# Elementwise work of keys, values, second layernorm and probability lows at fixed steps of VectorE, with GpSimd left to start transfers

## The chip, the core and the metric

The kernel runs on one core of a Trainium2 chip. The metric is the device time of one execution in microseconds (us); several executions are made, and their median is given. The profile names TensorE's matmuls PE and its weight loads PEld, VectorE DVE, ScalarE ACT, GpSimd POOL and SyncE SP.

## The reference

Sixteen sequences of 128 tokens, 1024 wide, pass through one block: cross attention behind a layernorm, then a linear layer with a routed low-rank addition behind a second layernorm.

```python
...
_layernorm(x) = (x - mean(x)) / sqrt(var(x) + 1e-05)
...
q = apply_rope((query @ Wq).reshape(b, t, 32, 128))
k = apply_rope((key @ Wk).reshape(b, t, 8, 128))
v = (value @ Wv).reshape(b, t, 8, 128)
logits = jnp.einsum('btkgd,bTkd->bkgtT', q, k) * ATTN_MULT
logits = MAX_ATTN_VAL * jnp.tanh(logits / MAX_ATTN_VAL)
logits = jnp.where(mask, logits, -1e+30)
attn = jnp.einsum('bkgtT,bTkd->btkgd', softmax(logits), v)
return attn.reshape(b, t, h * d) @ Wo
...
rw, sel = jax.lax.top_k(xf @ W_router.T, 2)
w = jnp.einsum('tk,tke->te', softmax(rw), onehot(sel))
lora = jnp.einsum('ter,te,eor->to', einsum('td,erd->ter', xf, A), w, B) * SCALING
return xf @ W_base.T + b_base + lora
...
x = x + cross_attention(_layernorm(x), ctx_4096, mask)
x = x + ffn(_layernorm(x))
```

## The kernel before, in words

All is float32. A product of two float32 matrices is made as three matmuls on rounded parts: each operand is split into a high part, copied by ScalarE into the type fp32r, and a low part, the float32 value less the high part, a subtraction on VectorE or GpSimd. `three()` (L233) issues high x high (L235), high x low (L236) and low x high (L237). So almost every tile that reaches TensorE costs one copy and one subtraction first, and elementwise work is spread over the three other engines.

The order of every engine is written out by hand. Each phase has a function per engine (`pe_kv`, `act_kv`, `dve_kv`, `pool_kv`, `sp_kv` and so on) that walks over the same job or step numbers; tables say which extra work stands at which number. `tick` counts a named semaphore up when an instruction ends, `wait_ge` makes an engine wait for such a count; every engine executes in order, so all that stands behind a waiting instruction waits too.

The 2048 tokens are four blocks of 512 columns (4 sequences each); `c` is the block.

**Keys and values (0 to some 325 us).** 56 jobs n of 24 matmuls write seven PSUM banks in turn. VectorE follows one or two jobs behind: the rotation of the keys (L386 to L400), the low part of the values (`vst`, L538), and the statistics of the first layernorm of x (`BN_STATS`, L547). `STATS`, `RS_A`, `RS_B`, `DIAG`, `SPREAD` say at which job number n the parts of that layernorm stand. `MASK` is 28: at this job TensorE makes a small product with the mask (L433) that is built into the bound `Bm` on the scores; VectorE has cast the mask before, at n = 26 (`mf`, `mr`, L591 and L593). `SUMS` are four instructions each on VectorE (L617 to L622), which add normalised blocks `Yx` of x in pairs to `T`, for a query product with seven products in place of eight. GpSimd makes the low part of the keys (`kst`) for the first eight pairs (`KPOOL`) and normalises the blocks `Yx` (one addition, L638, one multiplication, L643), and starts their stores to `XcD`. It has no job numbers there: each instruction runs as soon as its waits allow.

**Queries (some 328 us to the first attention steps).** The change leaves these functions as they are.

**Attention (some 960 to 1927 us).** 32 groups gi (four blocks c, eight key heads) of four query heads b. Steps `at` run from -16 to 255; a group takes eight steps. For head b of a group: scores, `tanh` on ScalarE, the minimum with `Bm` on VectorE (L1486), `exp` to `Pf`, copy to the high part `Ph`, low part `Pl` on GpSimd (L1528). At `DEN_AT` TensorE sums the probabilities of the group with a product with ones (L1291, 8 matmuls). The sums go through a transfer to `r`, a reciprocal on VectorE (L1498) one step later, a store to `rD` and a transfer `RB` per head that spreads the reciprocals over the partitions (L1519); all three are started by GpSimd. Five to ten steps behind the sums the products with the values are made, multiplied by `RB` (L1492), and split into `Ah` and `Al` (L1466). The same step of TensorE holds one job of the output product, 128x512, whose result VectorE adds into one of eight blocks of `Y` (L1479), with the job eight steps earlier in the same block. The weights of that product are 128x1024 pieces, split into `Rh` (L1216) and `Rl` (L1221).

In `dve_step` the order within a step is: low part of the queries `ql`, `Al`, addition into `Y`, minimum with `Bm`, product with `RB`, `Rl`, reciprocal.

**Second layernorm.** When a block c is done (every 64 steps), its layernorm is made during the next 64 steps, r = at % 64. `LN_LOAD` (4) to `LN_OUT` (38) are the values of r: sum over the rows (`ln_sum`), mean by a product with ones, subtraction of it (`ln_x`, L1790), squares on ScalarE, their sum (`ln_acc`, L1796), the root, one step of Newton (`ln_r`), multiplication (`ln_u`, L1813), and the split into high and low (`ln_xl`, L1774). GpSimd has 35 of these instructions per block, one `ln_x` per step and one `ln_u` every second step among them. The fourth block has the same steps squeezed into the jobs J of the second matrix product by `ln_last(J)`.

**Second matrix product (from 1928 us).** 40 jobs J of 24 matmuls, each with its router and low-rank parts. `r_lo` copies (L2033) a part of the router's weights that TensorE's first small product (L1885) needs.

```python
SUMS = {25: (0, 0), 26: (0, 1), 33: (0, 2), 35: (0, 3)}
KPOOL = 8
...
for d in (1, 2):
    if at - d in DEN_AT:
        gi = DEN_AT[at - d]
        for b in (2 * d - 2, 2 * d - 1):
            x = 4 * gi + b
```

Of the kernel before, what the change touches and what calls it, by code (L numbers as in the profile page):

```python
# [97 lines left out]
def program(nc, xT, xN, ctxT, gran, mask, bias, cst, dram, out):  # L98
    kD, vD, vE, qD, XcD, QSD, X2D, x1D, rD = dram
    ctx = ExitStack()  # L100
    with ctx:
# [259 lines left out]
        SUMS = {25: (0, 0), 26: (0, 1), 33: (0, 2), 35: (0, 3)}  # L361
# [5 lines left out]

        YLOAD = {2: 0}
# [131 lines left out]
        KPOOL = 8  # L500

        def k_low(t, u):

            for s in range(2):
                t.wait_ge("kv_kh", (u, s))
                t.e.tensor_tensor(kst[s][:, 1, :], kt[2 * (u % 2) + s][:, :], f(kst[s][:, 0, :]), ALU.subtract).then_inc(
                    *(t.tick("kv_kl", (u, s)) if u >= KPOOL else t.tick("kv_kp", (u, s))))

        def dve_kv(t):
# [5 lines left out]
            for n in range(-1, NK + 3):  # L515
# [78 lines left out]
                if n == MASK + 1:  # L594
# [30 lines left out]
        def pool_kv(t):  # L625
            e = t.e
            for u in range(KPOOL):
                k_low(t, u)
            for cp in range(1):
                for k, i in ((0, 0), (1, 0), (0, 1), (1, 1), (2, 0), (2, 1), (3, 0), (3, 1)):  # L630
                    b, s = xl0 if i == 0 else xl1
                    if (k, i) == (2, 0):
                        t.wait_ge("kv_lo", piece_of["W", 15])
                    for kk in (k, k + 4):
                        y = Yx[i][:, kk, :]
                        t.wait_ge(f"d_yx{i}{kk // 2}", cp)
                        t.wait_ge("kv_x", (2 * cp + i, 0))
                        e.tensor_tensor(y, y, b[:, :], ALU.add).then_inc(*t.tick("kv_xa", (cp, k, i, kk // 4)))  # L638
                    for kk in (k, k + 4):
                        y = Yx[i][:, kk, :]  # L640
                        t.wait_ge("kv_x", (2 * cp + i, 1))
                        t.wait_ge("kv_xa", (cp, k, i, kk // 4))
                        m = e.tensor_tensor(y, y, s[:, :], ALU.mult)  # L643
                        m.then_inc(*(t.tick("kv_xm", (cp, k, i)) if kk < 4 else t.tick("kv_xn", (cp, k, i))))
                    t.wait_ge("kv_xn", (cp, k, i))
                    for n, kk in ((0, k), (2, k + 4)) if i == 0 else ((6, k + 4),):
                        if k > 1:
                            t.wait_ge(f"d_xs{k % 2}{n}", (cp, k - 2))
                        e.dma_start(XcD[cp, n, :, k], Yx[i][:, kk, :]).then_inc(*t.tick(f"d_xs{k % 2}{n}", (cp, k), 16))
# [804 lines left out]
        def dve_step(t, at):  # L1454
# [38 lines left out]
            for x in [y for y in SPLIT.get(at, []) if at >= 0]:  # L1493
                w_low(t, x)
            if at - 1 in DEN_AT:
                gi = DEN_AT[at - 1]
                t.wait_ge(f"d_rt{gi % 2}", gi)
                e.reciprocal(r16[gi % 2][:, :], r16[gi % 2][:, :]).then_inc(*t.tick("a_rec", gi))  # L1498
            dve_ln(t, at)

        def pool_step(t, at):
# [19 lines left out]
            for d in (1, 2):  # L1521
                if at - d in DEN_AT:
                    gi = DEN_AT[at - d]
                    for b in (2 * d - 2, 2 * d - 1):
                        x = 4 * gi + b
                        t.wait_ge("a_ph", x)
                        t.wait_ge("a_den", gi)
                        e.tensor_tensor(Pl[x % NP][:, :], Pf[x % NP][:, :], f(Ph[x % NP][:, :]), ALU.subtract).then_inc(*t.tick("a_pl", x))  # L1528
# [6 lines left out]
            if 11 <= at < 19:  # L1535
                n = at - 11
                t.wait_ge("y_add", n + 8)
                t.wait_ge(f"d_y{n // 2}", 0)
                e.tensor_tensor(Y[:, n, :], Y[:, n, :], Y2[:, n, :], ALU.add).then_inc(*t.tick("y_x", n))
            pool_rows(t, at)  # L1540
            pool_ln(t, at)

        def pool_rows(t, at):
# [3 lines left out]
            if at - 2 < 0 or n < 0:  # L1547
                return
            o = at - 2 - n
            if n:  # L1550
                t.wait_ge("y_add", at - 2)
                if n == 1:
                    if c:
                        t.wait_ge("ln_u", (c - 1, 7))
                    else:
                        t.wait_ge("q_xm", (3, 3))
                    e.tensor_tensor(L2[:, :], Y[:, 0, :], Y[:, 1, :], ALU.add).then_inc(*t.tick("ln_sum", (c, 1)))
                else:
# [665 lines left out]
```

## Time and profile before

| | before |
|---|---|
| time, median of 3 runs | 2170.22 us (2169.26 to 2170.89) |
| the profiled execution | 2171.35 us |
| its span in the profile | 2169.6 us |
| granted clock of TensorE, mean | 0.997 |
| PE, PEld busy | 98%, 79% |
| DVE, ACT, POOL busy | 76%, 40%, 36% |
| DMA, mean rate | 234 GB/s |

The busy time is a sum over the whole span; it does not say whether the work was in anyone's way. A wait of an engine is given with the instruction that released it. Matmuls overlap in the timeline: one lasts some 0.4 us from its start to its end while the next starts earlier, so the pace is the distance of the starts. A granted clock of 1.0 is 2.4 GHz.

### The profile page before, as it was taken

The page shows a single profiled execution, that of the slowest core. Times are in us where ns is not written, and L with a number is a line of the kernel's source. Part 1 is how long each engine was busy: PE and PEld are TensorE (multiplying, and loading weights), DVE is VectorE, ACT ScalarE, POOL GpSimd, SP SyncE. Part 2 cuts the span into 40 slices and gives each one's busy share as a digit, 9 for nine tenths or more (in the row PEclk, how much of TensorE's full clock was granted, in tenths as well). Part 3 has the DMA queues.
Part 4 walks back from the last instruction along what each step waited for, and adds up shares of the span by engine and source line. Part 5 has one row for each costly group of instructions (what it writes and reads, how often), then busy time and mean ns, then how long its engine had stood idle before and what let it go on. Part 6 is the DMA issues. An engine that isn't in the chain of part 4 may idle for free.

```text
span 2169.6 us, 26526 instructions
## 1 busy us (share of the span) xinstructions
PE 2132.5 (98%) x9429; PEld 1723.6 (79%) x9429; DVE 1642.6 (76%) x2062; ACT 869.4 (40%) x1351; POOL 772.8 (36%) x761
## 2 busy tenths in 40 slices
PE   9998999999999999998999999999999999999999
PEld 7887887888788888876777777777777777888887
DVE  5957758898987666675777789898999989855533
ACT  3323333222241111146555556665565556423221
POOL 0371016555540000004533455445645554525300
PEclk9999999999999999999999999999999999999999
DMA  8678667777686565677655575578456855586861
GB/s 323 224 247 261 211 228 275 265 277 258 247 317 241 209 214 199 227 265 245 219 197 184 196 281 194 195 253 309 149 192 238 303 191 166 196 347 240 313 224 59
DMA packets 198532, 508.52 MB, mean 234 GB/s; under 512 B 20864, under 2 KB 46080, under 8 KB 196352
## 3 DMA queue, kind: packets, MB, share of 16 engines
q1 hardware_dynamic: 172160, 424.43, 55.3%
q0 software_dynamic: 26240, 82.38, 11.4%
q8 instruction: 76, 1.25, 0.2%
q14 instruction: 56, 0.46, 0.1%
HBM read 357.26 MB, written 149.16 MB: 233 GB/s over the span
## 4 chain that ended last, share of the span: by engine, by line
PE 85%; DVE 7%; issue 4%; DMA 2%; ACT 1%; POOL 1%; SPq 0%; DVEq 0%; ACTq 0%; POOLq 0%
PE pq L235 28%; PE pq L236 27%; PE pq L237 27%; PE pq L1291 1%; DVE ql L1373 1%; DVE Rl L1221 1%; DVE Y L1479 1%; DVE Al L1466 1%; DVE pq L1492 1%; DVE pq L1486 1%; DMA kraw<-ctxT 1%; POOL Pl L1528 0%; PE pq L1885 0%; DMA vD<-vst 0%; PE pq L1886 0%
## 5 line engine op out<-in xcount | busy, mean ns | idle before, releaser
L235 PE MATMUL pq<-Ah,Rh 128*128 128x512 f32 x1024 | 400.8, 391 | 7.4 <-DVE Y L1479 3.9
L237 PE MATMUL pq<-Ah,Rl 128*128 128x512 f32 x1024 | 399.3, 390 | 0.0
L236 PE MATMUL pq<-Al,Rh 128*128 128x512 f32 x1024 | 399.2, 390 | 0.0
L1221 DVE TENSOR_TENSOR Rl<-raw,Rh 128x1024 fp32r<-128x1024 f32 x176 | 274.0, 1558 | 122.3 <-ACT Rh L1216 121.9
L235 PE MATMUL pq<-Xq,qW 128*128 128x512 f32 x896 | 349.9, 391 | 4.9 <-issue 3.8
L236 PE MATMUL pq<-Xq,qW 128*128 128x512 f32 x896 | 349.3, 390 | 0.0
L237 PE MATMUL pq<-Xq,qW 128*128 128x512 f32 x896 | 349.2, 390 | 0.0
L1216 ACT ACTIVATE Rh<-raw 128x1024 fp32r<-128x1024 f32 x176 | 184.6, 1050 | 152.8 <-PE pq L237 119.7
L235 PEld LDWEIGHTS pq<-Ah,Rh 128*128 128x128 f32 x1024 | 192.6, 188 | 53.4 <-DVE Y L1479 5.8
L1534 POOL DMA_DIRECT2D r<-rT x32 | 22.9, 716 | 575.8 <-ACT rT L1402 575.8
L237 PEld LDWEIGHTS pq<-Ah,Rl 128*128 128x128 f32 x1024 | 192.5, 188 | 40.7
L236 PEld LDWEIGHTS pq<-Al,Rh 128*128 128x128 f32 x1024 | 192.7, 188 | 39.9
L235 PEld LDWEIGHTS pq<-Xq,qW 128*128 128x128 f32 x896 | 168.5, 188 | 42.9 <-issue 7.0
L237 PEld LDWEIGHTS pq<-Xq,qW 128*128 128x128 f32 x896 | 168.6, 188 | 35.2
L236 PEld LDWEIGHTS pq<-Xq,qW 128*128 128x128 f32 x896 | 168.6, 188 | 34.7
L1479 DVE TENSOR_TENSOR Y<-pq,Y 128x512 f32<-128x512 f32 x248 | 168.7, 681 | 34.8 <-PE pq L237 34.5
L869 ACT ACTIVATE qW<-qraw 128x512 fp32r<-128x512 f32 x96 | 60.6, 632 | 294.0 <-PE pq L237 267.2
L1373 DVE TENSOR_TENSOR ql<-qf,qh 128x512 fp32r<-128x512 f32 x128 | 174.6, 1365 | 0.0
L1528 POOL TENSOR_TENSOR Pl<-Pf,Ph 128x512 fp32r<-128x512 f32 x128 | 164.1, 1309 | 1.1
L1394 ACT ACTIVATE Ah<-pq 128x512 fp32r<-128x512 f32 x128 | 76.1, 594 | 141.7 <-DVE pq L1492 141.5
L1408 ACT ACTIVATE Pf<-pq 128x512 f32<-128x512 f32 x128 | 76.5, 598 | 117.8 <-DVE pq L1486 117.5
L1388 ACT ACTIVATE pq<-pq 128x512 f32<-128x512 f32 x128 | 74.9, 585 | 111.1 <-PE pq L237 110.7
(244 smaller groups left out, 4188.5 us busy)
## 6 DMA issues: line engine op xcount, KB each, us to landing
raw<-gran SPq DMA_DIRECT2D x177, 512.0 KB, 4.5
QSD<-qW SPq DMA_DIRECT2D x64, 512.0 KB, 3.4
qD<-qt SPq DMA_DIRECT2D x128, 256.0 KB, 5.5
qW<-QSD SPq DMA_DIRECT2D x64, 512.0 KB, 3.5
qf<-qD SPq DMA_DIRECT2D x64, 512.0 KB, 6.3
RB<-rD POOLq DMA_DIRECT2D x128, 256.0 KB, 4.9
qraw<-gran SPq DMA_DIRECT2D x48, 512.0 KB, 5.1
kD<-kst SPq DMA_DIRECT2D x32, 512.0 KB, 5.4
```

The source lines that it names most:

```text
L235: e.matmul(dst, lh, rh, start=first, stop=False, skip_group_check=more)
L236: e.matmul(dst, lh, rl, start=False, stop=False, skip_group_check=more)
L237: return e.matmul(dst, ll, rh, start=False, stop=last, skip_group_check=more)
L869: e.activation(q_place(u)[:, 0, :], q_source(u), ACT.Copy).then_inc(*t.tick("q_hi", u))
L1216: t.e.activation(piece(x)[1], raw[raw_of(x)][:, :], ACT.Copy).then_inc(*t.tick("w_hi", x))
L1221: t.e.tensor_tensor(l, raw[raw_of(x)][:, :], f(h), ALU.subtract).then_inc(*t.tick("w_lo", x))
L1373: t.e.tensor_tensor(v4(ql[x % 2][:, :]), qf[gi % 2][:, :, b * P:b * P + P], f(v4(qh[x % 2][:, :])), ALU.subtract).then_inc(*t.tick("a_ql", x))
L1388: e.activation(s, s, ACT.Tanh, scale=SCALE / CAP).then_inc(*t.tick("a_tanh", x))
L1394: e.activation(Ah[:, 4 * i:4 * i + 4, b * P:b * P + P], v4(ps[obank[x % 2]][:, :]), ACT.Copy).then_inc(*t.tick("a_ah", x))
L1408: e.activation(Pf[x % NP][:, :], s, ACT.Exp, scale=CAP).then_inc(*t.tick("a_exp", x))
L1479: e.tensor_tensor(Y[:, m, :], ps[ring_bank(n)][:, :], Y[:, m, :], ALU.add).then_inc(*t.tick("y_add", n))
L1528: e.tensor_tensor(Pl[x % NP][:, :], Pf[x % NP][:, :], f(Ph[x % NP][:, :]), ALU.subtract).then_inc(*t.tick("a_pl", x))
```

## The change

It moves 324 elementwise instructions of 128x512 from GpSimd to VectorE, each to a fixed step: 128 `Pl`, 16 `kst`, 32 on `Yx`, 8 additions of the residual into `Y` (`y_x`), and 140 of the second layernorm (the fourth block's too). GpSimd keeps the start of every transfer that it had. The first two `SUMS` go from jobs 25 and 26 to 26 and 27 and stand, as before, behind the mask casts in the code of one job number. `LN_OUT` goes from 38 to 39. The four `Pl` of a group stand 1, 2, 4 and 6 steps behind `DEN_AT` (1, 2, 2, 2 in the first three groups), ahead of the reciprocal. `ln_x` stand at r = 9, three at 11, and one each at 12 to 15. The last block's layernorm reaches to J = 22 instead of 17, and its reload starts at J = 24 instead of 22.

```diff
-        SUMS = {25: (0, 0), 26: (0, 1), 33: (0, 2), 35: (0, 3)}
+        SUMS = {26: (0, 0), 27: (0, 1), 33: (0, 2), 35: (0, 3)}
...
+        XBLOCK = {20: (0, 0), 21: (1, 0), 22: (0, 1), 25: (1, 1), 28: (2, 0), 29: (2, 1), 30: (3, 0), 31: (3, 1)}
...
-        KPOOL = 8
...
                     u = pair_of[KJ[n - 2][1:3]]
-                    if u >= KPOOL:
-                        k_low(t, u)
+                    k_low(t, u)
...
+                if n in XBLOCK:
+                    k, i = XBLOCK[n]
+                    m, s = xl0 if i == 0 else xl1
+                    for kk in (k, k + 4):
...
+                        e.tensor_tensor(y, y, m[:, :], ALU.add).then_inc(*t.tick("kv_xa", (0, k, i, kk // 4)))
+                    for kk in (k, k + 4):
...
+                        p = e.tensor_tensor(y, y, s[:, :], ALU.mult)
...
         def pool_kv(t):
             e = t.e
-            for u in range(KPOOL):
-                k_low(t, u)
...
+            for k, i in XBLOCK.values():
+                t.wait_ge("kv_xn", (0, k, i))
...
+                    e.dma_start(XcD[0, n, :, k], Yx[i][:, kk, :]).then_inc(*t.tick(f"d_xs{k % 2}{n}", (0, k), 16))
...
+        PL_AT = {}
+        for at, gi in DEN_AT.items():
+            for b, d in enumerate((1, 2, 2, 2) if gi < 3 else (1, 2, 4, 6)):
+                PL_AT.setdefault(at + d, []).append((gi, b))
...
                 w_low(t, x)
+            for gi, b in PL_AT.get(at, []):
+                x = 4 * gi + b
+                t.wait_ge("a_ph", x)
+                t.wait_ge("a_den", gi)
+                e.tensor_tensor(Pl[x % NP][:, :], Pf[x % NP][:, :], f(Ph[x % NP][:, :]), ALU.subtract).then_inc(*t.tick("a_pl", x))
             if at - 1 in DEN_AT:
...
+            if 11 <= at < 19:
...
+                e.tensor_tensor(Y[:, n, :], Y[:, n, :], Y2[:, n, :], ALU.add).then_inc(*t.tick("y_x", n))
+            if at == NT - 4:
+                r_lo(t, 0)
+            dve_rows(t, at)
             dve_ln(t, at)
...
-        LN_LOAD, LN_MEAN, LN_SQUARE, LN_SPLIT, LN_RSTD, LN_MORE, LN_OUT = 4, 8, 15, 25, 30, 36, 38
+        LN_LOAD, LN_MEAN, LN_SQUARE, LN_SPLIT, LN_RSTD, LN_MORE, LN_OUT = 4, 8, 15, 25, 30, 36, 39
+
+        LN_X = {9: (0,), 11: (1, 2, 3), 12: (4,), 13: (5,), 14: (6,), 15: (7,)}
...
-            if LN_MEAN + 1 <= r < LN_MEAN + 9:
-                k = r - LN_MEAN - 1
+            for k in LN_X.get(r, ()):
...
         def dve_ffn(t):
             e = t.e
-            r_lo(t, 0)
+            for at in (NT + 1, NT + 2):
+                dve_rows(t, at)
...
-                if J == 22:
+                if J == 24:
                     f_load(t, C - 1)
```

The order of the instructions on VectorE around the mask casts, before (`T` are the sums of `SUMS`, `vst` is the low part of a value job, `mf` and `mr` the casts of the mask):

```order
L549 BN_AGGR mv<-bnst 128x2
L617 TENSOR_TENSOR T_71<-Yx_68,Yx_67 128x512
L618 TENSOR_TENSOR T_73<-Yx_68 128x512
L620 TENSOR_TENSOR T_72<-Yx_68,T_71 128x512
L622 TENSOR_TENSOR T_74<-Yx_67,T_72 128x512
L538 TENSOR_TENSOR vst_106<-pq,vst_106 128x512
L547 BN_STATS bnst<-xn_70 128x6 x2
L549 BN_AGGR mv<-bnst 128x2
L591 CAST mf<-mu_107 128x128
L593 CAST mr<-mf 128x128
```

and with the change:

```order
L547 BN_AGGR mv<-bnst 128x2
L612 TENSOR_TENSOR Yx_68<-Yx_68,D_59 128x512 x2
L617 TENSOR_TENSOR Yx_68<-Yx_68,D_60 128x512 x2
L536 TENSOR_TENSOR vst_106<-pq,vst_106 128x512
L545 BN_STATS bnst<-xn_70 128x6 x2
L547 BN_AGGR mv<-bnst 128x2
L589 CAST mf<-mu_107 128x128
L591 CAST mr<-mf 128x128
L629 TENSOR_TENSOR T_71<-Yx_68,Yx_67 128x512
L630 TENSOR_TENSOR T_73<-Yx_68 128x512
L632 TENSOR_TENSOR T_72<-Yx_68,T_71 128x512
L634 TENSOR_TENSOR T_74<-Yx_67,T_72 128x512
```

The first `SUMS` are behind the casts now, and four instructions on `Yx`, which GpSimd had, are ahead of them.

VectorE in attention, around the reciprocal of a group, at r = 11 of a layernorm (`Y_158` is the block of `ln_x`, `r_56` the reciprocal), before:

```order
L1373 TENSOR_TENSOR ql_150<-qf_160,qh_148 128x512
L1479 TENSOR_TENSOR Y<-pq,Y 128x512
L1492 TENSOR_TENSOR pq<-pq,RB 128x512
L1221 TENSOR_TENSOR Rl_167<-raw_172,Rh_163 128x1024
L1498 RECIPROCAL r_56<-r_56 128x16
L1466 TENSOR_TENSOR Al<-pq,Ah 128x4x128
L1479 TENSOR_TENSOR Y<-pq,Y 128x512
L1486 TENSOR_TENSOR pq<-pq,Bm 128x512
```

and with the change:

```order
L1772 TENSOR_TENSOR Y_158<-Y_158,L_57 128x512 x3
L1372 TENSOR_TENSOR ql_150<-qf_160,qh_148 128x512
L1478 TENSOR_TENSOR Y<-pq,Y 128x512
L1491 TENSOR_TENSOR pq<-pq,RB 128x512
L1220 TENSOR_TENSOR Rl_167<-raw_172,Rh_163 128x1024
L1498 TENSOR_TENSOR Pl_185<-Pf_192,Ph_178 128x512
L1502 RECIPROCAL r_56<-r_56 128x16
L1772 TENSOR_TENSOR Y_158<-Y_158,L_57 128x512
L1465 TENSOR_TENSOR Al<-pq,Ah 128x4x128
L1478 TENSOR_TENSOR Y<-pq,Y 128x512
L1485 TENSOR_TENSOR pq<-pq,Bm 128x512
```

Between `Bm` and the reciprocal stand three `ln_x` and one `Pl` more, and a `Pl` or an `ln_x` stands in each step.

GpSimd over the same steps, before; of these rows those with DMA are left with the change:

```order
L1534 DMA r_56<-rT_153 128x1x16
L1790 TENSOR_TENSOR Y_158<-Y_158,L_57 128x512
L1528 TENSOR_TENSOR Pl_185<-Pf_192,Ph_178 128x512
L1528 TENSOR_TENSOR Pl_186<-Pf_193,Ph_179 128x512
L1790 TENSOR_TENSOR Y_158<-Y_158,L_57 128x512
L1509 DMA rD<-r_56 128x16
L1528 TENSOR_TENSOR Pl_187<-Pf_194,Ph_180 128x512
L1528 TENSOR_TENSOR Pl_188<-Pf_195,Ph_181 128x512
L1790 TENSOR_TENSOR Y_158<-Y_158,L_57 128x512
L1519 DMA RB<-rD 128x512 x4
L1790 TENSOR_TENSOR Y_158<-Y_158,L_57 128x512 x3
```

The chain from `r` over `rD` to `RB` has no arithmetic of GpSimd between its starts any more.

## Rows read from the trace of the kernel before

**Rows 1.** Page, part 1: busy us, share of span, instructions of each engine.
```profile
PE 2132.5 (98%) x9429; PEld 1723.6 (79%) x9429; DVE 1642.6 (76%) x2062; ACT 869.4 (40%) x1351; POOL 772.8 (36%) x761
```

**Rows 2.** Waits of TensorE: us in total, times, longest.
```profile
PE pq L433 <- DVE mr L593: 7.8, 1, 7.8
PE pq L235 <- DVE Y L1479: 3.9, 4, 1.2
...
PE pq L1885 <- DVE Rh L2033: 1.1, 1, 1.1
```

**Rows 3.** Timeline of VectorE, 156 to 172 us: start, us, engine, line, operation, names, shapes.
```profile
156.89 5.99 DVE L618 TENSOR_TENSOR T<-Yx 128x512 f32<-128x512 f32 x1
...
169.13 0.68 DVE L538 TENSOR_TENSOR vst<-pq,vst 128x512 fp32r<-128x512 f32 x1
...
171.36 0.23 DVE L593 CAST mr<-mf 128x128 fp32r<-128x128 f32 x1
171.51 0.68 DVE L617 TENSOR_TENSOR T<-Yx,Yx 128x512 f32<-128x512 f32 x1
172.11 0.69 DVE L618 TENSOR_TENSOR T<-Yx 128x512 f32<-128x512 f32 x1
```

**Rows 4.** Timeline of GpSimd, 156 to 163 us; x2: two in a row.
```profile
157.29 2.55 POOL L638 TENSOR_TENSOR Yx<-Yx,L 128x512 f32<-128x512 f32 x2
```

**Rows 5.** Groups of VectorE, shapes apart: busy us, mean ns, idle us before.
```profile
L1221 DVE TENSOR_TENSOR Rl<-raw,Rh 128x1024 fp32r<-128x1024 f32 x176 | 274.0, 1558 | 122.3 <-ACT Rh L1216 121.9
L1373 DVE TENSOR_TENSOR ql<-qf,qh 128x512 fp32r<-128x512 f32 x128 | 174.6, 1365 | 0.0
...
L1498 DVE RECIPROCAL r<-r 128x16 f32<-128x16 f32 x32 | 7.7, 242 | 13.0 <-DMA r<-rT 13.0
...
L1221 DVE TENSOR_TENSOR Vl<-raw,Vh 128x1024 fp32r<-128x1024 f32 x4 | 4.9, 1217 | 0.0
```

**Rows 6.** Timeline of TensorE, 171 to 172 us; in brackets the idle time before.
```profile
171.65 0.47 PE L433 MATMUL pq<-mr,ones 128*128 128x128 f32 x1 [7.79 <-DVE mr L593]
```

**Rows 7.** Two windows: us, busy (x) of PE, PEld, DVE, ACT, POOL, granted clock, DMA share.
```profile
160.00:180.00 20.00, 12.21 (x47) 9.66 (x46) 18.83 (x20) 5.15 (x8) 8.90 (x9) 0.83 0.54 183
180.00:200.00 20.00, 20.00 (x90) 16.57 (x89) 11.70 (x26) 6.19 (x8) 0.00 (x0) 1.00 0.86 261
```

**Rows 8.** Timeline of ScalarE, 156 to 158 us.
```profile
157.36 0.60 ACT L495 ACTIVATE vst<-pq 128x512 fp32r<-128x512 f32 x1 [4.90 <-DMA vD<-vst]
```

**Rows 9.** Chain that ended last: start, us, instructions; the ones products.
```profile
1057.03 1.00 PE pq L1291 x8
...
1114.40 1.00 PE pq L1291 x8
1142.83 1.00 PE pq L1291 x8
...
1864.33 1.00 PE pq L1291 x8
```

**Rows 10.** Timeline of TensorE, 1043 to 1053 us.
```profile
1043.43 0.47 PE L235 MATMUL pq<-Ah,Rh 128*128 128x512 f32 x1 [0.73 <-DVE Al L1466]
...
1052.41 0.50 PE L235 MATMUL pq<-Ah,Rh 128*128 128x512 f32 x1 [1.93 <-ACT Y L1415]
```

**Rows 11.** Timeline of all engines, 1332 to 1334 us.
```profile
1332.36 2.14 POOL L1519 DMA_DIRECT2D RB<-rD  x4 [0.73 <-DMA rD<-r]
...
1333.30 1.21 DVE L1221 TENSOR_TENSOR Rl<-raw,Rh 128x1024 fp32r<-128x1024 f32 x1
```

**Rows 12.** Timeline of VectorE, 1926 to 1928 us.
```profile
1926.79 0.69 DVE L1479 TENSOR_TENSOR Y<-pq,Y 128x512 f32<-128x512 f32 x1 [1.69 <-PE pq L237]
1927.40 0.18 DVE L2033 CAST Rh<-Rl 128x64 fp32r<-128x64 f32 x1
```

**Rows 13.** Timeline of VectorE, 1507 to 1508 us.
```profile
1507.60 0.70 DVE L1492 TENSOR_TENSOR pq<-pq,RB 128x512 f32<-128x512 f32 x1 [2.54 <-DMA RB<-rD]
```

More of the change, by code:

```diff
@@ L626, in pool_kv @@
             e = t.e
-            for u in range(KPOOL):
-                k_low(t, u)
[L629 to L649, printed above, removed]
+            for k, i in XBLOCK.values():
+                t.wait_ge("kv_xn", (0, k, i))
+                for n, kk in ((0, k), (2, k + 4)) if i == 0 else ((6, k + 4),):
+                    if k > 1:
+                        t.wait_ge(f"d_xs{k % 2}{n}", (0, k - 2))
+                    e.dma_start(XcD[0, n, :, k], Yx[i][:, kk, :]).then_inc(*t.tick(f"d_xs{k % 2}{n}", (0, k), 16))
             for c, half, b4 in v_jobs:
@@ L1520, in pool_step @@
             v_store(t, at)
[L1521 to L1528, printed above, removed]
             if at in DEN_AT:
@@ L1534, in pool_step, with dve_rows @@
                 e.dma_start(r16[gi % 2][:, :], rT[gi % 2][0:P:32, :]).then_inc(*t.tick(f"d_rt{gi % 2}", gi, 16))
[L1535 to L1539, printed above, removed]
             pool_rows(t, at)
             pool_ln(t, at)
+        def dve_rows(t, at):
+            e = t.e
+            c, n = (at - 2) // 64, (at - 2) % 64 - 56
+            if at - 2 < 0 or n < 1:
+                return
+            t.wait_ge("y_add", at - 2)
+            if n == 1:
+                if c:
+                    t.wait_ge("ln_u", (c - 1, 7))
+                else:
+                    t.wait_ge("q_xm", (3, 3))
+                e.tensor_tensor(L2[:, :], Y[:, 0, :], Y[:, 1, :], ALU.add).then_inc(*t.tick("ln_sum", (c, 1)))
+            else:
+                t.wait_ge("ln_sum", (c, n - 1))
+                e.tensor_tensor(L2[:, :], L2[:, :], Y[:, n, :], ALU.add).then_inc(*t.tick("ln_sum", (c, n)))
         def pool_rows(t, at):
@@ L1546, in pool_rows @@
             c, n = (at - 2) // 64, (at - 2) % 64 - 56
[L1547 to L1550, printed above, removed]
+            if at - 2 > 0 and n > 0 and n % 2:
                 t.wait_ge("y_add", at - 2)
[L1552 to L1558, printed above, removed]
-                    t.wait_ge("ln_sum", (c, n - 1))
-                    e.tensor_tensor(L2[:, :], L2[:, :], Y[:, n, :], ALU.add).then_inc(*t.tick("ln_sum", (c, n)))
-            if n % 2:
                 j = n // 2
@@ L1807, in pool_ln_step @@
                 e.tensor_tensor(L2[:, :], Dt[0][:, :], Dt[1][:, :], ALU.mult).then_inc(*t.tick("ln_r", (c, 2)))
+            if LN_OUT + 2 <= r < LN_OUT + 18 and (r - LN_OUT) % 2 == 0:
+                k = (r - LN_OUT) // 2 - 1
+                t.wait_ge("ln_xh", (c, k))
+                e.tensor_tensor(stg[k % 2][:, 1, :], Dt[k % 2][:, :], f(stg[k % 2][:, 0, :]), ALU.subtract).then_inc(*t.tick("ln_xl", (c, k)))
             if LN_OUT <= r < LN_OUT + 16 and (r - LN_OUT) % 2 == 0:
```

66 lines of the change are left out of this document (37 added, 29 removed).

## The prediction

> **What bounds the kernel now.** I read the page first: TensorE is busy 98% of the span [rows 1]. Shortening another engine's work therefore gains nothing by itself; only a stop of TensorE, or a stretch at its lower clock, can be won back. So the second view is TensorE's list of waits. Three entries bear on the change [rows 2]: 7.8 us once on VectorE's mask cast `mr`, 3.9 us in four waits on the accumulation `Y`, 1.1 us on the copy `Rh` at the start of the second matrix product. The rest stands in places that the change leaves alone.
>
> The third view says why VectorE was late. At the mask wait one subtraction of 128x512 whose operands both lie in SBUF took 5.99 us, while the same instruction 15 us later took 0.69, starting 0.60 after its neighbour [rows 3]. In those 5.99 us GpSimd ran one elementwise instruction of 1.3 us behind the other on the same kind of data [rows 4]. The same shows in the means: `Rl` takes 1558 ns where the like `Vl`, made while GpSimd rests, takes 1217, and `ql` takes 1365 [rows 5].
>
> **Part 1, keys, values and the mask.** TensorE would begin the mask product at 163.86 (171.65 less 7.79) [rows 6]. The wait costs more than its length: in the window that holds it 47 matmuls stand against 90 in the next and the granted clock is 0.83 [rows 7], so for some matmuls behind the stop TensorE ran at 1.2 instead of 2.4 GHz. 43 missing matmuls by 20/90 us are 9.6 us. The change takes all elementwise work off GpSimd there, and puts the first `SUMS` behind the mask casts in VectorE's order. What VectorE must then do between ScalarE's copy of value job 25, which ends at 157.96 [rows 8], and the end of `mr` is what it did from 169.13 to 171.59 [rows 3], 2.46 us. That gives 160.4, which is 3.4 us before TensorE comes. The four `Yx` instructions now ahead of it at step 25 (4 x 0.60 = 2.4 us) end before that copy does. If they and a late transfer met, up to 3.4 us would still be hidden. Term: **-9.6 us**, between -9.6 and about -4 (the casts late by 5 us more). The 16 `kst` instructions add 16 x 0.60 = 9.6 us to VectorE over the first 110 us; TensorE writes seven banks in turn there and VectorE follows one or two jobs behind, so I cost them at nothing. If that cover went, 9.6 us is the most. The transfers begun by GpSimd there keep their order and only come free of the arithmetic.
>
> **Part 2, attention.** The sum of ones products marks a period of the steady part: 28.43 us undisturbed (1114.40 to 1142.83). From the first shown, 1057.03, to the last, 1864.33, there are 28 periods, 796.0 us at that pace, and the three layernorm passes add 12 matmuls of 20/90 us, 2.7 us [rows 7]; 807.3 passed [rows 9]. So 8.6 us are lost there, more than the 3.9 us that the waits on `Y` say, because each stop also has a slow restart. What VectorE must do in a period, undisturbed, is four `Rl` of 1.22, 24 instructions of 0.60 (four each of `Bm`, `RB`, `Al` and `ql`, eight `Y`) and a reciprocal of 0.24, 19.5 us [rows 3, 5]. The change adds four `Pl`: 21.9. In the fullest periods of layernorm, 8 more instructions (`ln_u`, `ln_xl`, or `ln_x`, whose spread is the same) make 26.7 of 28.43 us, 94%. Over the kernel 324 instructions move, 324 x 0.60 = 194 us; what VectorE gets back is (1.558 - 1.217) x 176 + (1.365 - 0.69) x 128 = 146 us, and the smaller groups [rows 3, 5]. On average it is about as busy as now, but no single instruction lasts 5 us. TensorE needs an addition into `Y` only two steps (7.1 us) after VectorE may begin it, and the worst single step of the new order holds 4.5 us against 28.43 / 8 = 3.55, with lighter ones around it. So stops of this kind should end; I leave 1.6 us for new small ones. Term: **-7 us**, bounds -8.6 and 0.
>
> The start of attention does not gain. There VectorE waits for the broadcast `RB`, and TensorE stands 1.93 us at 1052.41 for what follows on it [rows 10]; this chain of transfers is started at the same events as before. Three `Pl` now lie ahead of `Al`, for which TensorE waited 0.73 us at 1043.43; they make that wait 1.8 us longer, and the 1.93 us behind it shorter by as much. Term 0, bounds -2 and +2. Beginning transfers costs GpSimd what it did, 2.14 / 4 = 0.53 us for each of four `RB` even beside a `Rl` of VectorE [rows 11].
>
> Here the Trainium skill speaks against the change: by "SBUF — State Buffer", section "SBUF: two separate sides", a VectorE instruction in a 2-port mode locks GpSimd out of writing descriptors, so that a start of some 620 ns takes 3100. It would hold for copies and casts; the same page, "Who interferes with whom", says that `tensor_tensor` stalled no transfer, and by that rule the trace agrees with its 0.53 us. By the first rule, were it to take in the moved instructions, three starts in a row per period (`r`, `rD`, `RB`) would make the chain 7 us longer (an estimate from that page).
>
> **Part 3, the second matrix product.** The 1.1 us on `Rh` [rows 2] do not go with the copy. VectorE's last `Y` ends at 1927.48 and the copy ran from 1927.40 [rows 12]; TensorE's first job there waits for that `Y` too. Term **-0.1 us**. The last layernorm pass is spread over steps 1 to 22 instead of 17, on a VectorE that has long waits there, and its reload begins at step 24, six steps before use. Term 0.
>
> **Sum.** -9.6 - 7 - 0.1 = -16.7. The profiled execution took 2171.35 us, 1.1 more than the median of the runs shown; against the median 2170.22 this gives 2153.5, and I say **2154**.
>
> **Rivals.**
> A, only the mask gains. VectorE executes in order, and each moved instruction has a wait of its own; the waits on ScalarE within one pass (`ln_acc` behind a square, `ln_xl` behind `stg`) could cost as much as the port gave back. For: 94% in full periods, and a wait of 2.54 us for `RB` already in the steady part [rows 13]. Against: moved instructions stand a step or more behind what they wait for. Time: 2170.2 - 9.6 = 2160.6.
>
> B, the mask wait stays in part (the value stores keep ScalarE's copy later than 157.96) while attention gains: -4 - 7, so 2159.
>
> C, slower: VectorE becomes the bound in the full periods. The place is the `RB` wait: the reciprocal now stands behind one more `Pl` and, in passes, `ln_x`, and the multiplication that needs `RB` is three steps later, with all of VectorE queued behind it. Two periods with `ln_x` and `ln_acc` and about 2.3 with `ln_u` in each of three passes are 13 periods with 1.7 us to spare. Each us of waiting beyond that costs 13 us. It decides from 1.7 + 16.7 / 13 = 3.0 us per period. At 4.5 us it gives 2170.2 - 16.7 + 13 x 2.8 = 2190. Against it: 2.54 us is the longest such wait in the steady part [rows 13], and it occurs once.
>
> D, a form of C by locked starts: if each of three starts waited for one `Rl` of 1.22 us, the chain would be 3.7 us longer, past C's deciding point: 2170.2 - 16.7 + 13 x 2.0 = 2179. The four starts of [rows 11] speak against it.
>
> E, nothing moves: the mask wait is replaced by another wait on the late DMA of the values and attention keeps its losses. Time: 2170, less the 0.1. Against it: behind the mask TensorE has its 90 matmuls and VectorE 8 of 20 us free [rows 7].
>
> **The numbers.** A measurement of this kernel tells about 0.2% (4.3 us) from no change. Chances: the forecast 0.63 (2150 to 2158), A 0.15, B 0.08, C 0.04, D 0.02, E 0.08. Faster by over 0.2% are forecast, A and B: 0.86. Within 0.2%: 0.08. Slower: 0.06. The range that holds 8 in 10 goes from 2150 (all 8.6 us of attention and 2 us of its start won, with the 9.6) to 2164 (A with 3.4 us of the mask wait left).
>
> **What would show it.** After the change no wait of TensorE on `mr`, and a granted clock of 1.0 around 160 to 180 us. `Rl` at a mean near 1220 ns and `ql` near 690, GpSimd's busy time 324 x 1.3 = some 420 us lower, VectorE's within some 50 us of now. The marks of the ones products spaced 28.4 us, and from first to last 800 us instead of 807. Still present: the stop at the start of the query part, the 1 us at the start of the second product, and together over 3 us around the `RB` wait of the third group. I am wrong if TensorE shows waits on `Y`, `Al` or `Rl` in the passes adding up to more than 3 us, if the wait on `mr` is over 1 us, or if VectorE's waits for `RB` rise above 3 us in a steady period.

## The result, and the profile after

| | before | changed | ratio, 95% interval |
|---|---|---|---|
| first comparison | 2170.55 us (4 runs) | 2148.86 us (2148.18 to 2150.67, 4 runs) | 0.9906, 0.9889 to 0.9922 |
| the same two again, beside the experiments | 2166.35 us (8 runs) | 2151.92 us (2149.62 to 2159.42, 5 runs) | 0.9940, 0.9921 to 0.9959 |

The kernel is faster by 14 to 22 us. The forecast was 16.7 us; its time, 2154, is 5.1 us above the 2148.86 us of the first comparison, and the low end of its range, 2150, lies 1.1 us above that. The 2151.92 us of the second comparison lie within the range. In the profiled execution the granted clock was 0.998 and the span 2148.9 us.

The page of the changed kernel, part 1 (busy us, share of the span, instructions), beside [rows 1]:

```profile
PE 2127.3 (99%) x9429; PEld 1723.2 (80%) x9429; DVE 1654.8 (77%) x2386; ACT 878.0 (41%) x1351; POOL 338.2 (16%) x437
```

GpSimd lost 434.6 us of busy time; VectorE took over 324 instructions and is busy 12 us longer in all. The groups of VectorE (busy us, mean ns), beside [rows 5], show why:

```profile
L1220 DVE TENSOR_TENSOR Rl<-raw,Rh 128x1024 fp32r<-128x1024 f32 x176 | 214.0, 1218 | 94.8 <-ACT Rh L1215 94.3
...
L1372 DVE TENSOR_TENSOR ql<-qf,qh 128x512 fp32r<-128x512 f32 x128 | 86.8, 680 | 0.0
```

`ql` went from 1365 to 680 ns, `Rl` from 1558 to 1218, which is the mean of `Vl` in [rows 5]. Of TensorE's waits (total, times, longest) `mr` and `Y` in attention are gone, against [rows 2]; `Y` instead of `Rh` now ends the wait ahead of the second product:

```profile
PE pq L235 <- DVE Al L1465: 2.0, 1, 2.0
...
PE pq L1891 <- DVE Y L1478: 0.8, 1, 0.8
```

The two windows of [rows 7], now with full clock and 90 matmuls in each:

```profile
160.00:180.00 20.00, 20.00 (x90) 16.54 (x89) 19.34 (x45) 6.15 (x10) 1.07 (x2) 1.00 0.83 276
180.00:200.00 20.00, 20.00 (x90) 16.56 (x89) 16.12 (x21) 9.47 (x10) 2.15 (x4) 1.00 1.05 344
```

The ones products of [rows 9], first and last of the same 29, from the chain that ended last. I call them the marks, and the time from the first to the last the mark stretch:

```profile
1046.16 1.00 PE pq L1290 x8
...
1845.11 0.99 PE pq L1290 x8
```

The span is 20.7 us shorter. The time splits as follows (starts of TensorE's instructions in the two traces):

| stretch | before | changed | difference |
|---|---|---|---|
| to TensorE's restart in the query part | 338.79 | 329.67 | -9.12 |
| to the first scores of attention | 618.80 | 618.98 | +0.18 |
| to the first of the marked ones products | 99.44 | 97.51 | -1.93 |
| between the marks, 28 periods | 807.30 | 798.95 | -8.35 |
| to the second matrix product | 63.51 | 63.21 | -0.30 |
| to the end of the span | 241.76 | 240.58 | -1.18 |

The restart is the first matmul behind a stop of over 2 us (2.36 and 2.21 us) that both kernels have early in the query part; the first query product itself starts at 328.10 and 319.14.

The last row is not work of the engines: from the start of the second product to the start of the last addition into `FY` it is 237.29 us in both. From the start of the final store to the end of the span it is 3.65 us before and 2.48 with the change.

### The profile page after: what moved, and what is told of

It is laid out like the page before. It is cut to its first block, busy times and chain, and to the rows that moved or that the text cites. A ratio compares the mean times of both kernels' runs of the same rounds, so it can differ in the third digit from the quotient of the medians.

```text
span 2148.9 us, 26502 instructions
## 1 busy us (share of the span) xinstructions
PE 2127.3 (99%) x9429; PEld 1723.2 (80%) x9429; DVE 1654.8 (77%) x2386; ACT 878.0 (41%) x1351; POOL 338.2 (16%) x437
## 4 chain that ended last, share of the span: by engine, by line
PE 93%; DMA 2%; DVE 2%; issue 2%; ACT 1%; SPq 0%; POOL 0%; ACTq 0%; DVEq 0%; POOLq 0%
PE pq L235 30%; PE pq L236 30%; PE pq L237 30%; PE pq L1290 1%; DMA kraw<-ctxT 1%; DMA QSD<-qW 0%; DMA RB<-rD 0%; DMA rD<-r 0%; PE pq L1891 0%; PE pq L1892 0%; DMA qD<-qt 0%; DVE Rl L1220 0%; DVE qW L877 0%; DVE Sq L774 0%; DVE Xq L741 0%
## 5 line engine op out<-in xcount | busy, mean ns | idle before, releaser
L1220 DVE TENSOR_TENSOR Rl<-raw,Rh 128x1024 fp32r<-128x1024 f32 x176 | 214.0, 1218 | 94.8 <-ACT Rh L1215 94.3
L1485 DVE TENSOR_TENSOR pq<-pq,Bm 128x512 f32<-128x512 f32 x128 | 88.8, 694 | 65.4 <-ACT pq L1387 64.6
L235 PE MATMUL pq<-F,Rh 128*128 128x512 f32 x288 | 112.9, 392 | 0.0
L237 PE MATMUL pq<-F,Rl 128*128 128x512 f32 x288 | 112.2, 390 | 0.0
```

The costliest lines, as they stand in the source:

```text
L235: e.matmul(dst, lh, rh, start=first, stop=False, skip_group_check=more)
L237: return e.matmul(dst, ll, rh, start=False, stop=last, skip_group_check=more)
L1220: t.e.tensor_tensor(l, raw[raw_of(x)][:, :], f(h), ALU.subtract).then_inc(*t.tick("w_lo", x))
L1485: e.tensor_tensor(v4(s), v4(s), bc(Bm[:, :].unsqueeze(1), [P, 4, P]), ALU.min).then_inc(*t.tick("a_min", x))
```

## The experiments

Twelve runs were made, in three groups of four; each group ran on a chip of its own, beside the kernel before. Without any loss the mark stretch is 28 x 28.43 + 2.7 = 798.7 us.

### The two halves of the change

**Keys and values alone.** The kernel before, with `kst`, `Yx` and `SUMS` as in the change (`XBLOCK`, no `KPOOL`); nothing of attention.

> Only the keys and values part of the change (kst, Yx, the first two SUMS one job later); attention and second layernorm stay on GpSimd. If the parts add up, TensorE has no wait on mr, the query phase starts 8.9 us earlier as in the changed kernel, and the time is 2170.5 - 9 = 2161.5, with the four waits on Y in the layernorm passes still there (3.9 us). If part of the gain there came only with the rest, less than 8.

Ratio 0.9961 (0.9943 to 0.9979), 2158.0 against 2167.0 us. There is no wait on `mr`; the restart in the query part comes at 329.05. Two waits on `Y` are there (0.55 and 1.24 us), not four as I expected, and the mark stretch is 802.87.

**Attention and layernorm alone.** The rest of the diff.

> Only the attention and layernorm part; the mask wait of 7.8 us stays. If the parts add up: 2148.9 + 9 = 2158, ones products from first to last 799 us instead of 807, and the stretch from the start of attention to the first of these marks 2 us shorter. My forecast of the part was 7 us (2163.5), with nothing at the start of attention.

Ratio 0.9962 (0.9946 to 0.9979), 2158.9 us. The wait on `mr` is 7.82 us, the mark stretch 798.95. By the medians the halves are worth 9.0 and 8.1 us; their sum, 17.1, lies between the 14.4 and the 21.7 us of the two comparisons.

### Which edit ends the mask wait

**Only the order.**

```diff
-        SUMS = {25: (0, 0), 26: (0, 1), 33: (0, 2), 35: (0, 3)}
+        SUMS = {26: (0, 0), 27: (0, 1), 33: (0, 2), 35: (0, 3)}
```

> The kernel before with only the first two SUMS at jobs 26 and 27, so behind the mask casts; all elementwise work stays on GpSimd. Theory order: what held the casts up was the four sums ahead of them, so the wait on mr goes and the time is 2161.5, as with the whole of the move. Theory shared access: with GpSimd still adding and multiplying, VectorE's four instructions between value job 25 and the end of the casts take up to 5 us each beside it, and a wait on mr of 1 to 6 us stays (2163 to 2169).

Ratio 0.9952 (0.9934 to 0.9969), 2154.95 us: as good as the whole move of keys and values. The timeline of VectorE (start, us) around the casts:

```profile
157.75 0.69 DVE L538 TENSOR_TENSOR vst<-pq,vst 128x512 fp32r<-128x512 f32 x1 [3.05 <-ACT vst L495]
...
159.79 2.27 DVE L591 CAST mf<-mu 128x128 f32<-128x128 uint8 x1
162.10 0.23 DVE L593 CAST mr<-mf 128x128 fp32r<-128x128 f32 x1
...
162.84 6.13 DVE L618 TENSOR_TENSOR T<-Yx 128x512 f32<-128x512 f32 x1
```

and TensorE's mask product, with no idle time ahead of it (the mark stretch stays at 803.33):

```profile
163.33 0.22 PE L433 MATMUL pq<-mr,ones 128*128 128x128 f32 x1
```

GpSimd still disturbs: the cast `mf` takes 2.27 us instead of 0.17, and a sum behind it 6.13. But what is ahead of the casts is short enough, and they end at 162.33, one microsecond before TensorE comes. Both theories had a part: the order ended the wait, and the instructions beside GpSimd stayed long.

**Only the move.** The changed kernel with `SUMS` back at jobs 25 and 26.

> The changed kernel with the first two SUMS back at jobs 25 and 26, ahead of the mask casts. Theory order alone: the wait on mr of nearly 8 us is back and the time is 2158. Theory shared access alone: on a VectorE without GpSimd beside it the four sums take 2.4 us, the casts end at 161.3 + 2.4 = 163.7 instead of 161.3, TensorE is there at about 163.3, so a wait of at most 1 us and a time within 2 us of the changed kernel. Then either of the two edits ends the wait.

Ratio 0.9912 (0.9882 to 0.9941), 2152.2 us, no wait on `mr`. VectorE:

```profile
157.08 0.69 DVE L629 TENSOR_TENSOR T<-Yx,Yx 128x512 f32<-128x512 f32 x1
157.68 0.69 DVE L630 TENSOR_TENSOR T<-Yx 128x512 f32<-128x512 f32 x1
158.28 0.69 DVE L632 TENSOR_TENSOR T<-Yx,T 128x512 f32<-128x512 f32 x1
159.00 0.69 DVE L634 TENSOR_TENSOR T<-Yx,T 128x512 f32<-128x512 f32 x1
...
161.86 0.23 DVE L591 CAST mr<-mf 128x128 fp32r<-128x128 f32 x1
```

and TensorE:

```profile
163.62 0.22 PE L434 MATMUL pq<-mr,ones 128*128 128x128 f32 x1
```

The four sums ahead of the casts take 0.69 us each, not up to 5.99, and the casts end 1.5 us before they are needed. So the change removed this wait twice over: it needed the long instructions beside GpSimd and the sums ahead of the casts together.

### Which edit ends the waits in attention

**Only `Pl`.** The kernel before with `PL_AT` and the 128 `Pl` in VectorE's step; the second layernorm stays on GpSimd.

> The kernel before with only the 128 Pl on VectorE. If the 2 us at the start of attention come from Pl (0.68 instead of 1.31 us each, and no collision), they are here: 2168.5, and outside the layernorm passes ql and Rl fall to 0.69 and 1.22 us. In the passes GpSimd still has 35 instructions per block and collides with a VectorE that has four more per group: the waits on Y stay or grow (theory shared access: 807 us between the first and last ones product, or more). If instead Pl on GpSimd caused the long ql in the passes too, 800 us and 2160.

Ratio 0.9960 (0.9947 to 0.9973), 2158.7 us; mark stretch 798.94, no wait on `Y`. The start of attention is no shorter (961.54 to 1061.61, 100.07 us), so I was wrong in what I expected there and in the layernorm passes.

**All but `Pl`.**

```diff
-            for gi, b in PL_AT.get(at, []):
...
-                e.tensor_tensor(Pl[x % NP][:, :], Pf[x % NP][:, :], f(Ph[x % NP][:, :]), ALU.subtract).then_inc(*t.tick("a_pl", x))
```

(The `Pl` are back in `pool_step`, as before.)

> The changed kernel with the 128 Pl back on GpSimd at their old place in its order; all the rest on VectorE. If Pl is what the waits on Y hang on, they come back in part, since Pl still collides four times per group, with ql or Rl of 2 to 5 us: 2 to 6 us slower than the changed kernel. If the sheer number of GpSimd's instructions in the passes (Pl and layernorm together) made the waits, either move alone removes them: 799 us between the first and last ones product here as well, and only the start of attention is up to 2 us longer.

Ratio 0.9926 (0.9908 to 0.9944), 2149.6 us. The marks:

```profile
1044.70 1.00 PE pq L1290 x8
...
1843.65 0.99 PE pq L1290 x8
```

798.95 us again. Either move alone is enough. (This kernel also keeps the layernorm's new steps, so it doesn't separate the engine of these instructions from their order.) The lengths of `ql` (min/median/max ns) before, with `Pl` alone moved, with `Pl` and the first `SUMS` moved (the two edits below), and with all but `Pl` moved:

```profile
L1373 DVE TENSOR_TENSOR ql<-qf,qh x128: 627/684/5941, 950.2 to 1850.7; 128x512 fp32r<-128x512 f32 x128
```

```profile
L1377 DVE TENSOR_TENSOR ql<-qf,qh x128: 622/681/2195, 953.5 to 1844.3; 128x512 fp32r<-128x512 f32 x128
```

```profile
L1377 DVE TENSOR_TENSOR ql<-qf,qh x128: 624/681/4641, 940.2 to 1828.7; 128x512 fp32r<-128x512 f32 x128
```

```profile
L1372 DVE TENSOR_TENSOR ql<-qf,qh x128: 626/681/3318, 940.7 to 1827.5; 128x512 fp32r<-128x512 f32 x128
```

The medians are the same; the mean falls from 1365 to 769, 778 and 757 ns, and the longest from 5.9 us to 4.6 or less. Which of these counts is seen at the waits. Before, the wait of 0.64 us on `Y` at 1333.43 comes behind two held `ql`:

```profile
1318.49 5.94 DVE L1373 TENSOR_TENSOR ql<-qf,qh 128x512 fp32r<-128x512 f32 x1
...
1329.18 3.00 DVE L1373 TENSOR_TENSOR ql<-qf,qh 128x512 fp32r<-128x512 f32 x1
```

In the four traces with the attention code as before (the kernel before twice, keys and values alone, only the order) there are ten waits on `Y`. Nine have such a pair ahead of them, 5.9 us and 3.0 us, 10.7 us apart; the tenth (1537.93) has a `Rl` of 5.27 and a `ql` of 2.97. A `ql` of 4.1 to 4.6 us by itself is followed by no such wait. Added up, `ql`, `Rl` and `Pl` ran over their undisturbed lengths by 7.5 us or more within 12 us ahead of each of the ten waits (7.3 us is the most without a wait behind it), and by at most 4.1, 5.0 and 2.6 us anywhere in the mark stretch of the three kernels with one part moved. So the loss hangs on delays that fall close together, and either move thins them out.

**Two edits only.** `SUMS` one job later and `Pl` on VectorE, on the kernel before: 128 of 324 instructions moved.

> The kernel before with only the two small edits of the last group together: the first two SUMS one job later, and the 128 Pl on VectorE; Yx, kst and the whole second layernorm stay on GpSimd. Theory two edits: no other part of the change moves the time, and this gives what the changed kernel gives, within 0.1%. Theory all of it: with the 35 instructions per block of the second layernorm on GpSimd the passes keep a loss, at least 2 us (0.1%) and up to 5.

Ratio 0.9920 (0.9901 to 0.9939), 2149.96 us (2147.26 to 2151.78). The marks:

```profile
1045.98 0.99 PE pq L1295 x8
...
1844.93 1.00 PE pq L1295 x8
```

These two edits give all that can be measured of the change (2151.92 us in the same group). The other 196 moved instructions bring nothing more that these runs can tell.

**The fixed steps without the move.** `Pl` on GpSimd at steps 1, 2, 4, 6 behind the sums in place of 1, 1, 2, 2.

> The kernel before with Pl still on GpSimd, but at the fixed steps of the changed kernel (1, 2, 4 and 6 behind the sums). Theory shared access: the waits on Y in the passes stay, 803 to 807 us between the first and last ones product. Theory fixed steps: what counts is that GpSimd's work is spread, and the waits go: 799 us, time 4 to 8 us lower. The mask wait stays in either case.

Ratio 1.0049 (1.0031 to 1.0066), 2179.2 us: slower by 11. Both theories had the marks wrong: they are 811.04 us apart. The start of attention has two waits on `Pl`, 7.7 us.

```profile
1063.49 1.00 PE pq L1295 x8
...
1874.53 0.99 PE pq L1295 x8
```

VectorE ahead of one of the waits on `Y`, and GpSimd at the same time:

```profile
1341.64 5.16 DVE L1377 TENSOR_TENSOR ql<-qf,qh 128x512 fp32r<-128x512 f32 x1
1346.73 0.68 DVE L1483 TENSOR_TENSOR Y<-pq,Y 128x512 f32<-128x512 f32 x1
```

```profile
1341.21 1.31 POOL L1797 TENSOR_TENSOR L<-L,D 128x512 f32<-128x512 f32 x1
1342.46 1.31 POOL L1529 TENSOR_TENSOR Pl<-Pf,Ph 128x512 fp32r<-128x512 f32 x1
1343.71 1.30 POOL L1797 TENSOR_TENSOR L<-L,D 128x512 f32<-128x512 f32 x1
1344.96 1.29 POOL L1529 TENSOR_TENSOR Pl<-Pf,Ph 128x512 fp32r<-128x512 f32 x1
```

`ql` begins at 1341.64, just behind the start of the first of four GpSimd instructions that follow one another without a gap, and ends at 1346.80, just behind the end of the last (1346.25). The addition into `Y` behind it comes late, and TensorE waits 0.49 us. TensorE's longest wait in the mark stretch is another, 1.66 us for `Pf` at 1499.37, behind a `ql` of 4.33 us and a `Rl` of 3.71. Spreading GpSimd's `Pl` between its layernorm instructions made the longest such rows longer (a `ql` of 6.92 us beside five) and only somewhat rarer (19 `ql` over 2 us in place of 23). Here the sum of the delays is no sure sign: behind the `ql` of 6.92 us at 1309.46 TensorE has no wait.

### The disputed mechanism by itself

**A dose.** The changed kernel with additions on GpSimd that nobody waits for.

```diff
+            e.memset(dz[:, :], 0.0).then_inc(*t.tick("dz", 0))
+            for i in range(60):
+                t.wait_ge("dz", i)
+                e.tensor_tensor(dz[:, :], dz[:, :], dz[:, :], ALU.add).then_inc(*t.tick("dz", i + 1))
```

> The changed kernel, with 60 useless additions of 128x384 on GpSimd at its start (a tile of its own that nobody reads; no engine waits for them). Theory shared access: while they run, VectorE's instructions whose two operands lie in SBUF (kRl, Xl, kst) take 2 to 6 us in place of 1.22 and 0.69, those that read PSUM (the rotation) stay at 0.68, and TensorE waits for Xl or kRl by several us more. Theory transfers or semaphores: nothing changes, since nothing depends on these additions.

The additions ran from 1.24 to 69.1 us, 1.13 us apart. VectorE's groups from 0 to 55 us in this kernel (count, busy us, mean ns):

```profile
L520 DVE TENSOR_TENSOR Al<-kraw,Ah 128x1024 fp32r<-128x1024 f32 x4 | 6.5, 1664 | 1.6 <-ACT Ah L474 1.6
...
L520 DVE TENSOR_TENSOR kRl<-kraw,kRh 128x512 fp32r<-128x512 f32 x4 | 4.8, 1236 | 0.2 <-ACT kRh L474 0.2
L506 DVE TENSOR_TENSOR kst<-kt,kst 128x512 fp32r<-128x512 f32 x4 | 4.4, 1124 | 7.8 <-ACT kst L481 7.7
...
L390 DVE TENSOR_TENSOR kt<-pq,cs 128x512 f32<-128x512 f32 x2 | 1.4, 678 | 0.0
```

and in the changed kernel without the dose:

```profile
L519 DVE TENSOR_TENSOR Al<-kraw,Ah 128x1024 fp32r<-128x1024 f32 x4 | 4.9, 1226 | 2.6 <-ACT Ah L473 2.5
...
L505 DVE TENSOR_TENSOR kst<-kt,kst 128x512 fp32r<-128x512 f32 x4 | 2.7, 690 | 9.8 <-ACT kst L480 9.7
L519 DVE TENSOR_TENSOR kRl<-kraw,kRh 128x512 fp32r<-128x512 f32 x4 | 2.7, 687 | 0.6 <-ACT kRh L473 0.5
...
L389 DVE TENSOR_TENSOR kt<-pq,cs 128x512 f32<-128x512 f32 x2 | 1.4, 680 | 0.0
```

Instructions with both operands in SBUF grow from 1226 to 1664, from 687 to 1236 and from 690 to 1124 ns; the rotation, which reads PSUM, stays at 678 to 680. No engine waits for the additions, so what slows VectorE here is access that it shares with GpSimd. The Trainium skill says this too ("SBUF — State Buffer", section "Who interferes with whom"): two SBUF inputs on VectorE contend with a GpSimd instruction that reads SBUF, and the second to come is blocked until the first has ended. The trace agrees as to who is slowed. It differs as to how long: the `ql` above waited for four GpSimd instructions, 4.6 us, not for one; in the dose, where each addition waits for a semaphore, VectorE lost only 0.43 to 0.55 us per instruction. The dose also differs in size (128x384) and reads one tile twice, so that the semaphore makes the difference is not shown. My expectation had the cause right and the size wrong: 2 to 6 us per instruction and several us more of waits did not come. The kernel ran once, in 2151.69 us, with the restart in the query part at 332.03, 2.4 to 3.0 us later than in the two traces of the changed kernel.

### Controls, and a further edit

**The changed kernel again.**

> The changed kernel again, beside the kernel before on the chip of this group: ratio 0.9906 as in the first comparison. In the last group the kernel before had a median of 2167.0, so some 2147; the sum of the two parts made there was 9.0 + 8.1 = 17.1, so 2150.

Its ratio is in the first table. Mark stretch 798.95; restart in the query part at 329.05.

**The kernel before again.**

> The kernel before, for a trace on the chip of these groups, where its median was 2166.4 and 2167.0 instead of 2170.5. If the lower time comes from the attention part: 803 us between the first and last ones product instead of 807.3, and 1 or 2 us in waits on Y instead of 3.9. If it comes from elsewhere: 807.

2164.8 us (2161.5 to 2169.7, 8 runs); ratio to the other executions of the same kernel 0.9983 (0.9963 to 1.0003). Its marks:

```profile
1054.66 0.99 PE pq L1291 x8
...
1857.54 1.00 PE pq L1291 x8
```

802.88 us, with two waits on `Y` (0.46 and 1.20 us) where the first trace had four. The two other traces with this attention code, keys and values alone and only the order, have 802.87 and 803.33. So this code loses 4.2 to 4.6 us in the steady part in three traces and 8.6 in one.

Between the two control traces (this one and the changed kernel again) the span is 15.0 us shorter: 9.74 to the restart, 0.98 to the first scores, -1.16 to the marks, 3.93 between them, 0.30 and 1.2 behind them. The first pair had 20.7. Of the 5.7 us between the two pairs 4.4 lie in the mark stretch and 3.1 at the start of attention, and 1.8 go the other way. That agrees with the 7 us by which the two comparisons differ; why executions differ so stays open.

**`Rl` ahead of the `RB` product in steps 0 to 7**, in the changed kernel:

```diff
-            for x in [y for y in SPLIT.get(at, []) if at < 0]:
+            for x in [y for y in SPLIT.get(at, []) if at < 8]:
```

(and `>= 8` at the later place). It aims at TensorE's longest wait in the trace of the changed kernel, and at the one behind it on VectorE:

```profile
1019.28 1.06 PE L1290 MATMUL pq<-Pf,ones 128*32 128x512 f32 x1 [2.36 <-DVE Rl L1220]
```

```profile
1017.41 0.70 DVE L1491 TENSOR_TENSOR pq<-pq,RB 128x512 f32<-128x512 f32 x1 [5.39 <-DMA RB<-rD]
1018.01 1.21 DVE L1220 TENSOR_TENSOR Rl<-raw,Rh 128x1024 fp32r<-128x1024 f32 x1
```

> The changed kernel with one more edit: in steps 0 to 7 VectorE makes Rl ahead of the minimum and the RB product, as in the steps below 0. In the changed kernel VectorE waits 5.39 us for RB at 1017.41 with Rl behind it, and TensorE waits 2.36 us for that Rl. If Rl is what TensorE lacks: that wait goes and the time is 2 us lower. If TensorE would next wait for Al of the same RB product (made 1.7 us after Rl): 0 to 1 us.

Ratio 0.9920 (0.9903 to 0.9937), 2149.8 us: no difference that can be told from the changed kernel. TensorE waits 2.20 us at the same place for `Pf` instead, which hangs on the same `RB` wait of VectorE.

## Why the prediction came out as it did

**The mask: right in size, incomplete in reason.** I forecast 9.6 us. The restart in the query part comes 9.12 us earlier in the first pair and 9.74 in the controls (338.79 to 329.05), the first query product 8.96 and 10.18 (328.10 to 319.14 and 317.92), clock included. I named two causes, GpSimd's arithmetic and the place of the first `SUMS`, and did not ask whether either alone would do. Both do. My sum for VectorE was 0.9 us off. The timeline of the changed kernel:

```profile
154.36 0.69 DVE L536 TENSOR_TENSOR vst<-pq,vst 128x512 fp32r<-128x512 f32 x1 [7.96 <-ACT vst L496]
...
156.41 1.24 DVE L612 TENSOR_TENSOR Yx<-Yx,D 128x512 f32<-128x512 f32 x2
157.56 1.28 DVE L617 TENSOR_TENSOR Yx<-Yx,D 128x512 f32<-128x512 f32 x2
158.77 0.69 DVE L536 TENSOR_TENSOR vst<-pq,vst 128x512 fp32r<-128x512 f32 x1
...
161.03 0.23 DVE L591 CAST mr<-mf 128x128 fp32r<-128x128 f32 x1
```

and ScalarE's copy of value job 25:

```profile
158.14 0.60 ACT L496 ACTIVATE vst<-pq 128x512 fp32r<-128x512 f32 x1 [3.81 <-DMA vD<-vst]
```

The casts end at 161.26, not 160.4. I had taken the end of that copy, 157.96, from the trace before; with the change it is 158.74, 0.8 us later, because the copy waited for a store of the values. The four `Yx`, which I had end before the copy, start only at 156.41 and end at 158.84, so VectorE was free for `vst` no earlier than 158.77 either; both delays have the same length, and the trace can't part them. TensorE came at 164.67, and 3.4 us of room were left.

**Attention: right in mechanism, short in size against the first trace.** I took 8.6 us as lost and left 1.6 for new small stops; there are none in the steady part. From [rows 9] to the marks above it is 8.35 us, and 0.25 remain. Against the kernel before on another chip it is 802.88 - 798.95 = 3.9 us. The term's bounds (0 to 8.6) hold both. What I did not see is that the 8.6 us is no property of the kernel but of one execution: three other traces with this code lost 4.2 to 4.6. Against those my 7 us is some 3 too much; that it came near the first pair is in part luck.

**The start of attention: no effect that can be told, as costed.** The 1.93 us in the table above can't be put down to the change. From the first scores to the first mark I read 99.44 and 96.35 us in the two traces of the kernel before, 97.51 and 97.51 in those of the changed one, 99.65 with only `SUMS` put back, 94.43 and 100.07 in two kernels in between. The waits move about within it: `Al` 2.00 us at 983.93, `Rl` 2.36 at 1019.28.

**The second product: 0.3 us instead of 0.1.** TensorE waits for `Y` there, as forecast:

```profile
1908.32 0.50 PE L1891 MATMUL pq<-F,Rh 128*128 128x512 f32 x1 [0.78 <-DVE Y L1478]
```

**What kept me 5 us above the time.** On the trace: 1.35 us too little in attention, 1.93 at its start, 1.18 in the last store, 0.2 ahead of the second product, against 0.66 too much up to attention (9.6 against 9.12 - 0.18); that makes 4.0, which is 20.7 - 16.7. The other 1.1 us is rounding (0.5) and that the profiled execution of the changed kernel lies 1.8 us above its median and that of the kernel before only 1.1. The start lies within the spread of the traces, and the low end of my range took in 2 us of it. The store I had not costed at all, and it goes with the edits: 3.65 us in the four traces in which GpSimd still has all its elementwise work (the kernel before twice, only the order, the fixed steps), 2.47 to 2.49 us in the other ten. Why is open.

**The rivals.** A (only the mask gains) and E (nothing) fell with the mark stretch of 799 us. B fell with the wait on `mr`. C needed waits for `RB` of over 3 us in thirteen periods; between 1060 and 1860 us the changed kernel shows one over 1 us, of 1.06. I argued against C that 2.54 us was the longest such wait before and came once; that reading was wrong, since the same trace has waits for `RB` of 2.97 us at 1279.29 and 2.64 at 1740.43. The change made them shorter, which I did not foresee. Of my three signs of being wrong none came: between 1060 and 1860 us TensorE waits on neither `Y` nor `Al` nor `Rl`. D fell too: GpSimd's starts of `RB` lasted no longer beside a VectorE with two SBUF operands in most instructions (duration min/median/max; before 536/538/558):

```profile
L1531 POOL DMA_DIRECT2D RB<-rD x128: 536/536/550, 978.1 to 1858.1; - x128
```

So the rule of the Trainium skill that I weighed against the change (a start held back by a 2-port instruction of VectorE) did not show in any of these 128 starts. By the same page ("SBUF — State Buffer", "Who interferes with whom") `tensor_tensor` has no such mode; the trace agrees in that no start was held. The page gives its 620 and 3100 ns for a whole transfer and not for its start, so my 7 us from them was rough.

## What to carry to other kernels

Find in the timeline the long instructions ahead of the one that makes TensorE late, and ask apart what overlaps them and what order they stand in: here either cure alone ended the mask wait, and either of two parts of GpSimd's load in attention, moved, ended the waits there. So try the smallest edit first; two of this change's many brought all of the gain. And take the loss that a change is to win back from more than one execution of the kernel before.

## What the runs showed that I had not expected

- VectorE can be held through a whole row of GpSimd instructions that follow one another without a gap: `ql` took 5.16 us beside four of them (1341.21 to 1346.25), and a sum 6.13 us in the run with only the order changed. It isn't always so: in the kernel before, beside five additions of the residual into `Y` without a gap (1075.17 to 1083.04), a `ql` took 1.23 us and a `Rl` 2.34. In the dose the loss was 0.43 to 0.55 us per instruction.
- The longest `ql` fell from 5.9 us to 2.2 with `Pl` moved (4.6 in the run of two edits) and to 3.3 with the layernorm moved, and either was enough: nine of ten waits on `Y` came behind a `ql` of 5.9 and one of 3.0 us close together, none behind one of 4.6 by itself.
- The same GpSimd instructions, only placed at later steps, made the kernel 11 us slower.
- The kernel before varied by 16.5 us in the last group (2160.9 to 2177.3 in 19 runs), and its steady part lost 4.2 and 8.6 us in its two traces.
- The last store, which no edit touches, took 1.2 us less in every kernel that has part of GpSimd's load moved.
- A stop of 4.5 us of TensorE on `qp` appears in the query part, which from the restart to the first scores lasted 4.0 to 6.5 us longer with it than in the first trace of the kernel before. It appears in three of the fourteen traces (the keys and values part alone, the `Rl` edit, the fixed steps), whatever the edit. It is part of the spread, and its cause stays open.
